# Largest values turned on TensorE, and routed rows in blocks of 128: a change to a cross-attention and mixture-of-experts kernel

## The reference, cut to what matters

```python
x = x + xattn(layernorm(x), ctx)   # 16 heads of 64; softmax over the 77 context rows; w_out, b_out
x = x + ffn(layernorm(x))          # 8192 rows

def ffn(x):                        # x2: 8192 rows of 128
    logits = x2 @ router_w.T       # 8 experts
    idx = top_k(softmax(logits), 2)
    gate = logits at the two chosen experts, 0 elsewhere
    for e in range(8):             # inner width 176
        y = (silu(x2 @ w1[e].T) * (x2 @ w3[e].T)) @ w2[e].T
        moe_out += gate[:, e] * y
    moe_out += (silu(x2 @ sw1.T) * (x2 @ sw3.T)) @ sw2.T      # a shared expert, all rows
```

## Time and profile before

| | us |
|---|---|
| median of 3 runs | 1169.38 |
| the profiled execution's own time | 1168.02 |
| its span, first to last instruction | 1166.2 |
| TensorE matmul busy | 996.5 (85%) |
| DVE busy | 845.5 (73%) |
| POOL busy | 685.6 (59%) |
| ACT busy | 634.1 (54%) |

### The profile page before, as it was taken

One profiled execution on the slowest core, in us unless ns is written; L12 is line 12 of the kernel. 1 busy time (PEld: TensorE's weight loads), 2 busy tenths in 40 slices (PEclk: granted clock), 3 DMA queues, 4 the chain that ended last, 5 costly groups with the idle time before them and its releaser, 6 DMA issues. The chain is left out here.

```text
span 1166.2 us, 28610 instructions
## 1 busy us (share of the span) xinstructions
PE 996.5 (85%) x9832; PEld 820.3 (70%) x9832; DVE 845.5 (73%) x1930; ACT 634.1 (54%) x1354; POOL 685.6 (59%) x995
## 2 busy tenths in 40 slices
PE   5867999999999999999999998778695886776782
PEld 5555888788788887778788886667494775654562
DVE  3676888989989989989989989935262453533654
ACT  3554887777777777777777776533141332222220
POOL 3223676657878787777778788753605224345354
PEclk9878999999999999999999999878796999887997
DMA  8152225333333333232343335424433533345443
GB/s 258 20 171 40 52 53 144 62 54 60 76 76 62 65 76 70 58 76 61 91 88 63 64 76 131 95 69 127 123 116 85 146 109 107 98 104 118 83 119 107
DMA packets 222733, 106.54 MB, mean 91 GB/s; under 512 B 160465, under 2 KB 214385, under 8 KB 221457
## 3 DMA queue, kind: packets, MB, share of 16 engines
q1 hardware_dynamic: 214400, 87.91, 31.9%
q0 software_dynamic: 8192, 16.79, 5.2%
HBM read 38.59 MB, written 34.60 MB: 63 GB/s over the span
## 5 line engine op out<-in xcount | busy, mean ns | idle before, releaser
L583 POOL DMA_INDIRECT w_raw<-ys,pos_y x128 | 121.5, 949 | 191.0 <-DVE X L1103 119.5
L522 POOL TENSOR_TENSOR O_lo<-O,O_hi 128x512 f16<-128x512 f32 x128 | 147.4, 1171 | 143.6 <-ACT O_hi L677 143.6
L1007 DVE TENSOR_TENSOR pt_lo<-Q,pt_hi 77x512 f16<-77x512 f32 x256 | 164.1, 679 | 44.3 <-ACT pt_hi L669 43.7
L669 ACT ACTIVATE pt_hi<-Q 77x512 f16<-77x512 f32 x256 | 144.5, 590 | 31.8 <-PE Q L1255 31.2
L473 POOL DMA_INDIRECT xs<-x2cat,pos x128 | 133.7, 1045 | 34.3 <-issue 33.8
L1255 PE MATMUL Q<-ident,P 128*77 128x128 f32 x1024 | 149.0, 279 | 1.4 <-ACT P L652 0.7
L1189 PE MATMUL S<-G,xTm 128*128 128x462 f32 (+1 forms) x384 | 145.3, 514 | 0.6 <-ACT G L659 0.6
L646 ACT ACTIVATE v_hi<-W 77x512 f16<-77x512 f32 x128 | 76.1, 596 | 124.5 <-PE W L1133 116.7
L1242 PE MATMUL S<-v_hi,pt_hi 96*128 96x65 f16 x1024 | 112.5, 198 | 31.3 <-DVE P L976 28.9
L1242 PEld LDWEIGHTS S<-v_hi,pt_hi 96*128 96x128 f16 x1024 | 95.6, 98 | 49.0 <-DVE P L976 41.6
L1255 PEld LDWEIGHTS Q<-ident,P 128*77 128x77 f32 x1024 | 122.8, 150 | 2.5 <-issue 1.5
(11 more groups left out here) (255 smaller groups left out, 2916.1 us busy)
## 6 DMA issues: line engine op xcount, KB each, us to landing
ys<-ysb SPq DMA_DIRECT2D x44, 256.0 KB
xg_early<-xs SPq DMA_DIRECT2D x60, 128.0 KB
xp<-x2cat SPq DMA_DIRECT2D x64, 64.0 KB, 1.9
y_out<-X SPq DMA_DIRECT2D x16, 256.0 KB
xg_late<-xs SPq DMA_DIRECT2D x28, 128.0 KB
xs<-zero_in SPq DMA_DIRECT2D x24, 128.0 KB, 2.5
X<-x_in SPq DMA_DIRECT2D x1, 2304.0 KB, 9.9
xs<-x2cat,pos POOLq DMA_INDIRECT x128
```

The source lines that it names most:

```text
L522: pool.tensor_tensor(O_lo[:, half_], O[:, (t + 1) % 2, half_], O_hi[:, half_], ALU.subtract).then_inc(s["p_Olo"], 1)
L583: pool.indirect_dma_start(out=Yr[:, q % YR, k, i * D:(i + 1) * D], out_offset=None, in_=ys_d[batch_part(b)][:, :], in_offset=index(pos_y, ...
L669: act.activation(pt_hi[0:NK, j % 2, c * 512:(c + 1) * 512], QB[q_bank(j, c)][0:NK, :], ACT.Copy).then_inc(s["a_PThi"], 1)
L1007: dve.tensor_tensor(pt_lo[0:NK, j % 2, c * 512:(c + 1) * 512], QB[q_bank(j, c)][0:NK, :], pt_hi[0:NK, j % 2, c * 512:(c + 1) * 512], ALU.s ...
```

## The change

- **Largest values.** The three `partition_all_reduce` are gone. Largest values of context, `wv` and `wo` are taken together in slot -1 (`largest_set`), turned by one TensorE transpose (`amax_turn`), reduced and masked to powers of two by DVE in three partitions (`powers`), and spread to all partitions by a small matmul (`amax_spread`). The same helpers serve `w1`, `w3`, `w2` in slots 9 and 10; their largest values are taken in nine thirds in slots 0 to 8, and the split of `w1` and `w3` moves from slots 5 to 10 to slots 11 to 16. `wv` is no longer scaled before its split: ACT makes `wv_hi` and POOL `wv_lo` at the start, and the scale is applied in `v_high` and `v_low`. `wo` is split in slots 0 and 1.
- **Blocks of 128.** `GRAN` = 128, four blocks in a group (`PER` = 4). Padding falls: `ROUTED` = 14, 14, 10, which is 38 routed groups, `NI` = 54. `add_at` becomes 22, 25, 28, ... 58, 61, 64.
- **Packed words.** The table holds one word per group with the four experts (4 bits each) and two words with four block numbers (8 bits each). TensorE and SP load the words and take them apart with register arithmetic.
- The order of the first loads, and the slots of two loads of x, move.

```diff
-GRAN = 256
-PGRAN = [2 * (-(-(2 * NQ * n // GRAN + E - 1) // 2)) for n in PART]
+GRAN = 128
+PER = GB * NQ // GRAN
+PGRAN = [PER * (-(-(2 * NQ * n // GRAN + E - 1) // PER)) for n in PART]
@@ pool
-            pool.wait_ge(s["amax_done"], 4)
-            nc.gpsimd.partition_all_reduce(amall[:, :], amax[:, :], 128, bass.bass_isa.ReduceOp.max).then_inc(s["amax_all"], 1)
+            pool.wait_ge(s["wv_hi_done"], 1)
+            pool.tensor_tensor(wv_lo[:, :], wv_raw, wv_hi[:, :].bitcast(F), ALU.subtract).then_inc(s["wv_lo_done"], 1)
...
-                if t == 1:
-                    pool.wait_ge(s["amax_o_done"], 1)
-                    nc.gpsimd.partition_all_reduce(amax_o[:, 1:2], amax_o[:, 0:1], 128, ...)
-                if t == 4:
-                    pool.wait_ge(s["amax_f_done"], 3)
-                    nc.gpsimd.partition_all_reduce(amall_f[:, 0:3], amax_f[:, 0:3], 128, ...)
@@ vector
+            def powers(n):
+                dve.wait_ge(s["m_turn"], n)
+                dve.tensor_reduce(low3[0:3, 0:1], WB[2][0:3, T_AMAX:T_AMAX + 128], AX.X, ALU.max).then_inc(s["m_low"], 1)
+                dve.wait_ge(s["m_low"], 2 * n - 1)
+                dve.tensor_scalar(low3[0:3, 1:2], low3[0:3, 0:1], TINY, None, ALU.max).then_inc(s["m_low"], 1)
+                dve.wait_ge(s["m_low"], 2 * n)
+                dve.tensor_scalar(wide3[0:3, :].bitcast(U), low3[0:3, 1:2].bitcast(U).broadcast_to([3, 128]), 0x7F800000, None,
+                                  ALU.bitwise_and).then_inc(s["m_wide"], 1)
...
-                    dve.tensor_tensor(v_lo[...], WB[k][...], v_hi[...], ALU.subtract)
+                    dve.scalar_tensor_tensor(v_lo[...], WB[k][...], sc[0:NK, 6:7], v_hi[...], ALU.mult, ALU.subtract)
...
+                if t == -1:
+                    largest_set()
+                    powers(1)
...
+                if on(t, 2, S_AMAX + 1):
+                    ffn_largest(t)
@@ tensor
+            def amax_turn(n, of, ready):
+                pe.wait_ge(s[ready], 1)
+                if n == 1:
+                    pe.wait_ge(s["a_G"], 4 * (GB - 1) + 1)
+                pe.transpose(WB[2][0:3, T_AMAX:T_AMAX + 128], of[:, 0:3], ident[:, :]).then_inc(s["m_turn"], 1)
+
+            def amax_spread(n):
+                pe.wait_ge(s["m_wide"], n)
+                pe.matmul(WB[2][:, T_POW:T_POW + 3], wide3[0:3, :], ident[0:3, 0:3], start=True, stop=True).then_inc(s["m_pow"], 1)
...
-                at = nc.values_load_multi_w_load_instructions(tab[0:1, p, first:first + 2], engines=(mybir.EngineType.PE,),
-                                                              min_val=0, max_val=E * 128)[1]
-                return [(q * GRAN, GRAN, v) for q, v in enumerate(at)]
+                word = nc.values_load_multi_w_load_instructions(tab[0:1, p, first:first + 1], engines=(mybir.EngineType.PE,),
+                                                                min_val=0, max_val=0x8888)[1][0]
+                return [(q * GRAN, GRAN, pe.snap(((word >> 4 * q) & 15).with_bounds(min_val=0, max_val=E) * 128)) for q in range(PER)]
@@ sync, load_rows
-                    for q, v in enumerate(at):
-                        sp.dma_start(rows_in(n)[:, 2 * q:2 * q + 2, :],
+                    blocks = [b.with_bounds(min_val=0, max_val=XROWS // GRAN - 1) * GRAN for w in words for b in (w & 255, w >> 8)]
+                    for q, v in enumerate(blocks):
+                        sp.dma_start(rows_in(n)[:, q:q + 1, :],
```

More of the change, by code:

```diff
@@ L40 @@
 K_THR = K_CAP + E
-K_TRI = K_THR + NTHR
+K_PE = K_THR + NTHR
+K_SP = K_PE + PER
+K_TRI = K_SP + 2
 K_IOTA = K_TRI + E * E
 NKC = K_IOTA + max(PGRAN)
-ROUTED = [g // 2 for g in PGRAN]
+ROUTED = [g // PER for g in PGRAN]
 NR = sum(ROUTED)
+T_EDGE = 3 * max(PGRAN) // 4
 NS = NB // GB
@@ L118, in program @@
         amax = sb("amax", [128, 4])
[L119 to L122, removed]
+        am3 = sb("am3", [128, 4])
+        amax_f = sb("amax_f", [128, 3, 3])
+        am3_f = sb("am3_f", [128, 4])
+        low3 = sb("low3", [4, 2])
         sc = sb("sc", [128, 8])
@@ L286, in rows_loaded @@
         def rows_loaded(eng, n):
-            eng.wait_ge(s[f"xg{n % XG}"], sum(32 if m < NR else 16 for m in range(n % XG, n + 1, XG)))
+            eng.wait_ge(s[f"xg{n % XG}"], sum(16 * PER if m < NR else 16 for m in range(n % XG, n + 1, XG)))
         PACE = 2.75
@@ L343, in clear_edges @@
                     at = nc.values_load_multi_w_load_instructions(
-                        tab[0:1, p, 2 * max(PGRAN) + i * per:2 * max(PGRAN) + (i + 1) * per], engines=(mybir.EngineType.SP,),
+                        tab[0:1, p, T_EDGE + i * per:T_EDGE + (i + 1) * per], engines=(mybir.EngineType.SP,),
                         min_val=0, max_val=E * CAP - GRAN)[1]
@@ L357, in load_rows @@
                     p = part_of(n)
-                    first = 2 * (n - first_of(p))
+                    first = n - first_of(p)
                     if first == 0:
@@ L615, in _ @@
                     context_high(FIRST)
+            act.wait_ge(s["ld_wv"], 16)
+            act.activation(wv_hi[:, :], wv_raw, ACT.Copy).then_inc(s["wv_hi_done"], 1)
             def turn_out(t):
@@ L645, in v_high @@
                         wait(act, "s_O", 3 * (t - 1))
+                    if t == 0:
+                        act.wait_ge(s["scale_step"], 3)
                     act.activation(v_hi[0:NK, j % 2, 8 * k:8 * k + 8, 0:DH],
-                                   WB[k][0:NK, :].rearrange("p (h n) -> p h n", h=8), ACT.Copy).then_inc(s["a_Vhi"], 1)
+                                   WB[k][0:NK, :].rearrange("p (h n) -> p h n", h=8), ACT.Copy,
+                                   scale=sc[0:NK, 6:7]).then_inc(s["a_Vhi"], 1)
                 def exps(p):
@@ L908, in tables @@
                 e_i, low_i, row = (one[:, at:at + g] for at in (32, 96, 160))
-                big, big_1 = f[:, 256:], one[:, 256:]
+                big, big_1 = f[:, 320:], one[:, 320:]
                 past = big_1[:, 0:g * E].rearrange("p (i e) -> p i e", e=E)
@@ L1011, in slot @@
                     residual(t - 1)
+                if t == 0:
+                    scales()
                 if on(t, 0, NB):
                     piece_max(0); piece_max(1); piece_sub(0); piece_max(2); piece_sub(1); piece_sub(2)
-                if t == 2:
-                    dve.wait_ge(s["wo_hi_done"], 1)
-                    dve.scalar_tensor_tensor(wo_lo[:, :, :], wo_raw.rearrange("p (c n) -> p c n", c=8), so[:, 3:4],
-                                             wo_hi[:, :, :], ALU.mult, ALU.subtract).then_inc(s["wo_lo_done"], 1)
                 if on(t, 0, NB):
@@ L1277, in slot @@
                     turn(t)
+                if t == -1:
+                    amax_turn(1, am3, "amax_all")
+                if t == S_AMAX + 1:
+                    amax_turn(2, am3_f, "amax_f_all")
+                if t == S_AMAX + 2:
+                    amax_spread(2)
                 if gon:
                     g_piece(3)
+                if t == -1:
+                    amax_spread(1)
                 if now:
```

181 lines of the change are left out of this document (88 added, 93 removed).

## The result

The kernel after takes **1187.49 us** (median of 4 runs, 1183.89 to 1191.85) beside 1169.06 for the kernel before on the same chip: ratio 1.0153, 95% interval 1.0111 to 1.0195. It is slower by 18 us where 14 us faster was predicted. Its profiled execution took 1185.89 us (span 1183.9), 17.9 above that of before.

The account below looks back on a forecast made before the run. It took TensorE to pace the slots, all-reduce waits the start, and TensorE's work plus gather bursts the groups, with its sequencer pacing routed groups afterwards. 1168 - 27 + 3 + 10 = 1154, plus 1.4: 1155 us, range 1141 to 1168.

Parts of the forecast that it names:

- Start, -27: Start and first slots: removing the all-reduces saves 7 us before batch 0 and net 20 in slots 0 to 7.
- Slots, +3: Middle slots: scaled low part of the values +1 us and longer table operations +2; bounds 0 and 8.
- 128 of them at 0 to +0.02: +1: Slots: DVE's 128 `v_low` operations, now with the scale, each cost 0 to 0.02 us more, 1 us in all.
- +1 us per part: Slots: wider table operations add 1 us per part, with two parts in the slots, so 2 us.
- loads run four groups ahead: Groups: SP's four loads and arithmetic, some 4.5 us per group, stay under 5.6, late only while edges are cleared.
- Groups, 5.6 us per routed group: Routed groups: TensorE's sequencer, with doubled address operations and unpacking, takes 5.6 us, above TensorE's own 4.2.
- Sums of the groups, +10: From 765 us to the end: 165 + 126 + 84 + 36 = 411 us where 401 were measured before.
- TensorE's columns per group stay: Groups: 36 products of 128 columns replace 18 of 256, leaving TensorE's own work per group unchanged.
- The burst, "6.3": Groups: eight indirect DMAs of POOL cost 6.3 us per burst, one burst in 2.75 groups.
- The tail, 36: After the last group: three bursts of 10 us left, 3 landing and 3 adds, 36 us where 27 before.
- The second: Rival for routed groups: unpacking takes 1.5 us instead of 0.5, 6.6 us per group, 1188 us; chance 0.17.
- The first, 1118: Rival for routed groups: sequencer work stays hidden, groups stay at 4.2 us, 1118 us in all; chance 0.24.

Follow-up runs that it names:

- e5: Kernel before with only the largest-value and start edits, values copied and subtracted without the scale: 1141.19 us, ratio 0.9782.
- e11: Kernel before with only the largest-value and start edits, value weights scaled once in place after slot 3's values: 1144.02 us, ratio 0.9792.
- e2: Kernel before with only blocks of 128, packed words and their tables; start unchanged: 1208.83 us, ratio 1.0311.
- e6: Kernel after, row loads of the first four groups issued one group per slot in slots 60 to 63: 1179.47 us, ratio 1.0128.
- e3: Kernel after, TensorE taking routed expert weights from addresses fixed at build time, no word loaded or address computed: 1150.18 us, ratio 0.9804.
- e8: Kernel after, all four blocks of a group taking the expert of its first block: 1154.28 us, ratio 0.9891 to before.
- e9: Kernel before, routed up products issued in halves of 128 columns, next group's address load moved behind the down products: 1179.42 us, ratio 1.0107.
- e16: Kernel after, TensorE's table holding four values per group, loaded one by one and not unpacked: 1084.34 us, ratio 1.0295 to before.
- e4: Kernel before, blocks of 256 kept, each routed up product issued in two halves of 128 columns with one address: 1203.06 us, ratio 1.0249.
- e19: Kernel before, unchanged, run again where gather bursts were cheap: 1052.09 us.
- e18: Kernel after, unchanged, run again where gather bursts were cheap: 1074.99 us, ratio 1.0208 to before.

## Why the prediction was wrong, by its own steps

- **Start, -27.** Right: -27.5 by slot 13, with scores of batch 0 at 24.4 for 24.5. The detail differs: 32.3 by slot 7, and 4.8 back in slots 7 to 13, where the thirds and splits of the expert weights now are, which were to cost nothing there.
- **Slots, +3.** Wrong, and the first half of the miss: 17.7 from slot 13 to the first of the silu line, where the bound was 8. "128 of them at 0 to +0.02: +1" was a mis-sized term and left ACT out: the scale makes ACT's high part 88 ns and DVE's low part 61 ns longer, 5 us in all (e5, e11). Tables, "+1 us per part": 5 us in slots 36 to 48 for the first part alone (e2), though DVE's table operations there grew by only 2.6 us (8.5 for 5.9); one slot alone takes 15.2 us for 11.5. And "loads run four groups ahead" overlooked that these four groups are loaded in slot 60 in front of `turn_heads`: 5 us (e2; e6 takes them away). The last 2.4, between slot 63 and the silu line, stay open: e6, with the loads spread, still takes 31.9 us there, after 31.5 and before 29.1.
- **Groups, 5.6 us per routed group.** Right: 5.75 (rival: 4.2), and e3 and e8 show that it is register work. Unpacking, 0.5, was 0.65 to 0.8.
- **Sums of the groups, +10.** Wrong, +27.5, the second half of the miss: 173, 214 and 42 us for 165, 126 + 84 and 36. Absorbing was not what failed: "less about 10 absorbed" is what e3 and after show ahead of the first add. Three terms failed.
  - "TensorE's columns per group stay" put 36 small products for 18 at nothing. Until the first add e3, without any register work and with two groups fewer, takes 148.9 us from its first silu, where two groups fewer leave 142.4 of the 150.8 of before: 6.5 us that the sum lacked. e9 and e3 show the same in the period, 1.7 us.
  - The burst, "6.3", was read from the one step that it makes longest (10.5 - 4.2). The steps beside it are longer too: three groups with one burst take 20.3 us in before, 7.7 above three undisturbed ones, and 7.5 above in after. Over 16 groups at 2.75 per burst that is 7 to 8 us, and the 16 took 134 where 126 was forecast. The prediction had the sign of it: its own formula gave 6.5 us per group where 6.9 was measured.
  - The tail, 36, was 42. Three gathers were left, as forecast, but the first starts 3.5 us after the last silu, and the second lasts 11.8 us until the third begins.
- **Sum.** -27.5 + 17.7 + 27.5 = +17.7, the difference of the spans, for -27 + 3 + 10 = -14.
- **Rivals.** The second gave 1188 by an unpacking of 1.5 us; the time came out there by chance, the cause didn't (e16). The first, 1118, had a true core (36 small products run at 4.3 with fixed addresses), but six groups fewer give 8 us and not 27. The clock barely moved (0.924 for 0.929). The real case, right pace and too cheap surroundings, was not among the rivals; its time lay 7 us above the range. And by its own signs of being wrong, pace and start, the prediction would have passed: none of them looked at the slots or at the groups that meet a burst.

## What to carry to other kernels

Count what the sequencer passes, not only what the engine multiplies. Here each address from a register costs it an operation of 0.11 us, and three products need two: 0.23 us, against 0.33 us of TensorE at 256 columns and 0.17 at 128. With the smaller blocks the sequencer sets the pace. Halving products also halves what is queued behind a blocking register load, so put such loads where the queued instructions are long. A scale folded into an operation that runs in every slot is not free; fold a power of two into the weights once. Take the price of a disturbance from a whole period, not from its longest step.

## What the runs showed of the hardware

- 16 to 17 pairs of weight load and product were still to start on TensorE when its sequencer began to load a register (e4, in five groups in a row); at 128 columns they last 0.93 us, and that is all the cover there is.
- While eight indirect DMAs of POOL run (10 us in most gathers, up to 12 in the tails), TensorE starts about 140 instructions, at the usual pace for the first 4 to 10 us and then mostly one every 0.71 us, in before and after alike. But that is not a constant: three groups with one burst take 20.3 us of before in the profiled run of this case and 13.9 in e19, where three undisturbed ones take 12.6, and the steps of 0.69 to 0.73 us between two TensorE instructions are 51 in the one and 4 in the other. Chip 12 showed both (before 1172.47 and 1053.37 us), so it isn't a property of the chip, as the expectation of e18 supposed. What it depends on was not found.
- ACT's copy of 77x512 from PSUM takes 597 ns without and 685 ns with a scale per partition; DVE's subtraction there 679 ns, and 740 with the scale in it.
